# Turning base_w on VectorE instead of TensorE in the last expert of a two-layer MoE kernel

## The reference

```python
# layer 0: per-sample 128x128 matrix, then a top-8 of 64 experts MoE (I = 384, capacity 256)
y = einsum('bct,bcd->bdt', x, weights[conditions])
h = silu(inp @ wg[e]) * (inp @ wu[e]);  out = h @ wd[e]        # for each of 64 experts
# layer 1: a dense layer with an adapter, then a dense layer with router and 8 LoRA experts
c = x @ W.T + s[a] * (x @ A[a].T) @ Bm[a].T
f = c @ base_w.T + base_b + 2 * sum_e gate_e * (c @ lora_A[e]) @ lora_B[e],  gate from c @ router_w.T + router_b
```

## Time and profile before

| | |
|---|---|
| median of 3 runs | 2366.0 us (2363.48 to 2366.01) |
| the profiled execution: time, span | 2365.02 us, 2363.3 us |
| PE busy | 2326.7 us, 98% of the span |
| DVE, ACT, POOL busy | 75%, 60%, 57% of the span |
| granted PE clock, mean | 0.995 |
| chain that ended last: PE | 94% of the span |
| experts' period | 25.0 us each |
| composition stage (L931) | 1791.6 to 1907 us |
| DMA | 582 MB, mean 246 GB/s |

### The profile page before, as it was taken

How to read it: one execution, slowest core, us unless ns; L and a number is a source line. 1 busy time by engine, 2 the same in 40 slices (tenths; PEclk the granted TensorE clock), 3 DMA queues, 4 the chain that set the end, 5 groups by cost and what they waited for, 6 DMA issues and landing times.

```text
span 2363.3 us, 35497 instructions
## 1 busy us (share of the span) xinstructions
PE 2326.7 (98%) x12594; PEld 2044.4 (87%) x12594; DVE 1780.2 (75%) x3091; ACT 1418.5 (60%) x2349; POOL 1343.8 (57%) x999
## 2 busy tenths in 40 slices
PE   6989999999999999999999999999999999999999
PEld 4768788888888888888888888888889999999999
DVE  4887788888888888888888888888863267666665
ACT  4766677777767777777777776777763122222221
POOL 4117888777777777877778777787730011111110
PEclk9999999999999999999999999999999999999999
DMA  8999899989999989989899899899886444544452
GB/s 300 380 311 335 257 281 288 287 272 292 279 289 290 281 276 283 286 280 279 276 291 282 275 285 279 281 282 287 274 255 140 103 110 131 144 131 132 132 140 83
DMA packets 250307, 582.35 MB, mean 246 GB/s; under 512 B 82697, under 2 KB 106634, under 8 KB 250130
## 3 DMA queue, kind: packets, MB, share of 16 engines
q1 hardware_dynamic: 183154, 401.18, 51.6%
q0 software_dynamic: 55584, 160.02, 26.2%
q10 hardware_dynamic: 11392, 18.88, 2.1%
HBM read 456.25 MB, written 123.45 MB: 245 GB/s over the span
## 4 chain that ended last, share of the span: by engine, by line
PE 94%; DVE 2%; issue 2%; ACT 1%; DMA 1%; ACTq 0%; POOL 0%; SPq 0%; DVEq 0%; POOLq 0%
PE ps L861 26%; PE ps L874 22%; PE ps L860 13%; PE ps L986 9%; PE ps L979 7%; PE ps L931 5%; PE ps L857 4%; PE ps L730 2%; PE ps L969 2%; PE ps L858 2%; PE ps L740 1%; PE ps L943 1%; PE ps L753 1%; PE ps L752 0%; ACT HR L1215 0%
## 5 line engine op out<-in xcount | busy, mean ns | idle before, releaser
L861 PE MATMUL ps<-XX,HR 128*128 128x512 f32 x2688 | 959.7, 396 | 0.0
L632 POOL DMA_INDIRECT Xg<-yd,idx x504 | 659.3, 1308 | 161.1 <-issue 152.7
L860 PE MATMUL ps<-XX,LR 128*128 128x256 f32 x2688 | 750.4, 279 | 0.1
L1747 DVE TENSOR_TENSOR LR<-raw,HR 128x1536 fp32r<-128x1536 f32 x384 | 657.8, 1751 | 10.1 <-ACT HR L1215 9.1
L861 PEld LDWEIGHTS ps<-XX,HR 128*128 128x128 f32 x2688 | 505.1, 188 | 104.2
L1215 ACT ACTIVATE HR<-raw 128x1536 fp32r<-128x1536 f32 x384 | 557.0, 1478 | 22.5 <-DMA raw<-in_L_ffn_wd 17.5
L860 PEld LDWEIGHTS ps<-XX,LR 128*128 128x128 f32 x2688 | 507.6, 189 | 18.3 <-DVE LR L1747 0.7
L654 POOL DMA_INDIRECT accd<-ot,toki x128 | 252.9, 1976 | 150.0 <-ACT ot L1269 127.8
L874 PE MATMUL ps<-LR,hH 128*128 128x512 f32 x768 | 303.3, 395 | 0.0
L874 PE MATMUL ps<-HR,hH 128*128 128x512 f32 x768 | 299.8, 390 | 3.0 <-DVE hL L1793 2.2
L874 PE MATMUL ps<-HR,hL 128*128 128x512 f32 x768 | 301.8, 393 | 0.0
(11 more groups left out here) (252 smaller groups left out, 3869.1 us busy)
## 6 DMA issues: line engine op xcount, KB each, us to landing
raw<-in_L_ffn_wd SPq DMA_DIRECT2D x128, 768.0 KB
raw<-in_L_ffn_wg SPq DMA_DIRECT2D x126, 768.0 KB
raw<-in_L_ffn_wu SPq DMA_DIRECT2D x126, 768.0 KB
yd<-yrow ACTq DMA_DIRECT2D x32, 512.0 KB
x<-accd SPq DMA_DIRECT2D x32, 512.0 KB, 3.9
out<-x SPq DMA_DIRECT2D x31, 512.0 KB, 5.2
xt<-in_x SPq DMA_DIRECT2D x25, 512.0 KB
accd<-xt SPq DMA_DIRECT2D x25, 512.0 KB
```

The costliest lines, as they stand in the source:

```text
L632: eng.indirect_dma_start(Xg[:, c, q, :], None, yd4, bass.IndirectOffsetOnAxis(ap=idx4[:, e % 4, i:i + 1], axis=0))\
L860: eng.matmul(bank(out, 0, CAP), wl, xx[:, 0:CAP], start=False, stop=False)
L861: mm = eng.matmul(bank(out), wh, xx, start=False, stop=(k == 7))
L1747: eng.tensor_tensor(LR[:, (n + 2) % NHL, :], raw[:, n % NRAW, :], HR[:, (n + 2) % NHL, :].bitcast(F32), ALU.subtract).then_inc(s_L, 1)
```

## The change

base_w is no longer turned by PE. SP loads each of its eight row blocks in four DMAs of 32 partitions (rows of 1 KB), DVE turns each block with one stream transpose (32x32 blocks, as the token stage does), and the same order of the contraction index is given to W, Bm, lora_A and router_w by splitting their loads in the same way. The first four row blocks are loaded into Xg and XR, right behind the last expert's last weights; the landings are waited for in pairs of blocks (`d_bw[j // 2]` at 128). In the last expert DVE turns blocks 0 to 3 ahead of split dB and of the join of block 189, blocks 4 and 5 ahead of join 190, blocks 6 and 7 ahead of low_w(0) and join 191. High and low parts of whole blocks (128x1024) are written after the last low_h, and the results of expert 63 after the high parts. The first composition block works its columns in thirds (384, 384, 392), each waiting for its own low parts. The composition's banks are swapped with those of the token stage's start. In the token stage the low planes of tile 4 are written before two `low_T`, `take(p, 1)` of the first fast pair before two `turn_r`, and `sums` gets one more wait.

The diff, cut to its core:

```diff
-        BK = {"G1": 0, "G2": 1, "A": 2, "B": 4, "C": 5, "D": 6}
+        BK = {"G1": 4, "G2": 5, "A": 6, "B": 0, "C": 1, "D": 2}
...
+CF = [(0, 384), (384, 768), (768, NX)]
...
+        def base_in(j):
+            if j < 2:
+                return Xg[:, j, :, :].rearrange("p q s -> p (q s)")
+            if j < 4:
+                return XR[:, j - 2, :, :, :].rearrange("p q j t -> p (q j t)")
+            return x1[:, j - 4, :] if j < 6 else x45[:, j - 6, :]
...
+            def load_b(j):
+                for f in range(4):
+                    eng.dma_start(base_in(j)[32 * f:32 * f + 32, :].rearrange("s (q c) -> s q c", q=4),
+                                  base_w[j * P:(j + 1) * P, f * 256:(f + 1) * 256].rearrange("(q s) c -> s q c", q=4))\
+                       .then_inc(d_bw[j // 2], 16)
...
                 load_unit(n)
+                if n == len(units) - 1:
+                    eng.wait_ge(s_vl, 2 * E)
+                    for j in range(4):
+                        load_b(j)
...
-                        eng.dma_start(laR[:, :, e, :],
-                                      lora_A[e].rearrange("(q p) r -> p q r", p=P)).then_inc(d_la, 16)
-                        eng.dma_start(bmR[:, :, e, :],
-                                      Bm[e].rearrange("(q p) r -> p q r", p=P)).then_inc(d_la, 16)
+                        for f in range(4):
+                            p4 = slice(32 * f, 32 * f + 32)
+                            eng.dma_start(laR[p4, :, e, :],
+                                          lora_A[e].rearrange("(f j i) r -> f i j r", f=4, j=8)[f]).then_inc(d_la, 16)
+                            eng.dma_start(bmR[p4, :, e, :],
+                                          Bm[e].rearrange("(f j i) r -> f i j r", f=4, j=8)[f]).then_inc(d_la, 16)
...
-                        eng.dma_start(wr(k)[:, :, 32 * f:32 * f + 32],
-                                      W.rearrange("(q p) d -> p q d", p=P)[:, :, c:c + 32]).then_inc(d_wr[k % 2], 16)
+                        for h in range(4):
+                            eng.dma_start(wr(k)[32 * h:32 * h + 32, :, 32 * f:32 * f + 32],
+                                          W.rearrange("(h j i) d -> h i j d", h=4, j=8)[h][:, :, c:c + 32])\
+                               .then_inc(d_wr[k % 2], 16)
...
-            eng.wait_ge(s_dn, 4 * (E - 1))
-            for j in range(3):
-                load_b(j)
             eng.wait_ge(s_L, len(units) - 2)
-            eng.dma_start(x1[0:NA, 2, :], router_w).then_inc(d_bw[3], 16)
-            load_b(3)
             load_b(4)
+            load_b(5)
+            with nc.allow_non_contiguous_dma(reason="128-byte runs"):
+                for f in range(4):
+                    eng.dma_start(x1[0:NA, 2, :].rearrange("a (j f i) -> a j f i", j=8, f=4)[:, :, f],
+                                  router_w.rearrange("a (f j i) -> f a j i", f=4, j=8)[f]).then_inc(d_rw, 16)
             eng.wait_ge(s_L, len(units))
-            for j in range(5, 8):
-                load_b(j)
+            load_b(6)
+            load_b(7)
             eng.wait_ge(s_bf, 1)
             load_w(0)
-            eng.wait_ge(s_bf, 17)
+            eng.wait_ge(s_bl, 6)
             load_w(1)
+            eng.wait_ge(s_bl, 10)
...
-                        if e == E - 1:
-                            for n in ([o], [4 + 2 * o, 5 + 2 * o], [12 + o])[j]:
-                                turn_b(n)
+                        if e == E - 1 and j == 0 and o == 0:
+                            turn_router()
...
-                if j == 0:
-                    eng.wait_ge(s_bl, 10)
-                    eng.wait_ge(s_out, 4 * E - 1)
+                if j == 1:
+                    eng.wait_ge(s_out, 4 * E)
...
+                if j == 0:
+                    eng.wait_ge(s_gs, 3 * E)
+                    for g, (a, z) in enumerate(CF):
+                        eng.wait_ge(s_bl, (4, 7, 10)[g])
+                        for q in range(8):
+                            for m, (X, Y) in enumerate([(WH, BH), (WH, BL), (WL, BH)]):
+                                mm = eng.matmul(bank(b0 + g, 0, z - a), X[:, 0, q, :], Y[:, q, a:z],
+                                                start=(q == 0 and m == 0), stop=(q == 7 and m == 2))
...
-            for n in range(12):
-                high_b(n)
+            high_router()
+            for j in range(7):
+                high_b(j)
+            eng.activation(BH[:, :, D + NA:NX], laR[:, :, :, :].rearrange("p q a r -> p q (a r)"), ACT.Copy)\
+               .then_inc(s_bh, 1)
+            high_b(7)
             for o in range(4):
                 result(E - 1, o // 2, o % 2)
-                high_b(12 + o)
-            high_b(16)
...
+            def turn_b(j):
+                eng.wait_ge(d_bw[j // 2], 128)
+                if j >= 5:
+                    eng.wait_ge(s_bt, j)
+                eng.transpose(base_t(j), base_in(j)).then_inc(s_bt, 1)
+
+            def low_b(j):
+                eng.wait_ge(s_bh, j + 2 if j < 7 else 10)
+                eng.tensor_tensor(base_dst(BL, j), base_4(j), base_dst(BH, j).bitcast(F32), ALU.subtract)\
+                   .then_inc(s_bl, 1)
...
+                if e == E - 1:
+                    eng.wait_ge(s_dn, 4 * (E - 1))
+                    turn_b(0)
+                    turn_b(1)
+                    turn_b(2)
+                    turn_b(3)
+                    split("dB", e)
                 join(3 * e)
...
                 low_h(3 * e)
-                split("dB", e)
+                if e < E - 1:
+                    split("dB", e)
+                else:
+                    turn_b(4)
+                    turn_b(5)
                 join(3 * e + 1)
...
+                    turn_b(6)
+                    turn_b(7)
                     low_w(0)
                 join(3 * e + 2)
...
-            for n in range(17):
-                eng.wait_ge(s_bh, n + 2)
...
+            eng.wait_ge(s_bh, 1)
+            eng.tensor_tensor(BL[:, :, D:D + NA], bank(0, 0, 64).rearrange("p (q a) -> p q a", q=8),
+                              BH[:, :, D:D + NA].bitcast(F32), ALU.subtract).then_inc(s_bl, 1)
+            for j in range(7):
+                low_b(j)
+            eng.wait_ge(s_bh, 9)
+            eng.tensor_tensor(BL[:, :, D + NA:NX], laR[:, :, :, :].rearrange("p q a r -> p q (a r)"),
+                              BH[:, :, D + NA:NX].bitcast(F32), ALU.subtract).then_inc(s_bl, 1)
+            low_b(7)
...
                 eng.wait_ge(s_xr, 2 * p + 2)
+                if p == ND:
+                    eng.wait_ge(s_sL, 4)
...
             gate_of(3)
+            low_r(4, 0)
+            low_r(4, 1)
+            low_g(3)
             low_T(2)
-            low_g(3)
             low_T(3)
             final(1, "G2")
             final(1, "D")
-            low_r(4, 0)
-            low_r(4, 1)
...
+                take(p, 1)
                 if p == ND:
                     turn_r(t1 + 2)
                     turn_r(t2 + 2)
-                take(p, 1)
```

More of the change, by code:

```diff
@@ L906, in _ @@
                 down(e)
-            turn_b(16)
             for j in range(9):
@@ L925, in _ @@
                 b0 = mbank(j)
[L926 to L932 removed]
+                if j == 0:
+                    eng.wait_ge(s_gs, 3 * E)
+                    for g, (a, z) in enumerate(CF):
+                        eng.wait_ge(s_bl, (4, 7, 10)[g])
+                        for q in range(8):
+                            for m, (X, Y) in enumerate([(WH, BH), (WH, BL), (WL, BH)]):
+                                mm = eng.matmul(bank(b0 + g, 0, z - a), X[:, 0, q, :], Y[:, q, a:z],
+                                                start=(q == 0 and m == 0), stop=(q == 7 and m == 2))
+                else:
+                    for q in range(8):
+                        for m, (X, Y) in enumerate([(WH, BH), (WH, BL), (WL, BH)]):
+                            for g, (a, z) in enumerate(CG):
+                                mm = eng.matmul(bank(b0 + g, 0, z - a), X[:, j % 2, q, :], Y[:, q, a:z],
+                                                start=(q == 0 and m == 0), stop=(q == 7 and m == 2))
                 mm.then_inc(s_m, 1)
```

99 lines of the change are left out of this document (32 added, 67 removed).

## The result

The changed kernel takes 2370.4 us (median of 19 runs, 2366.5 to 2375.8) where the kernel before, on the same chip, takes 2365.4 (19 runs, 2362.1 to 2368.6): a ratio of 1.0023, 95% interval [1.0017, 1.0030]. The forecast was 2369.0 with a range of 2359 to 2374. It is slower by 4.9 us between medians; the forecast's sum was 2.9 slower.

The account below looks back on a forecast made before the run. TensorE, busy for 98% of the span, was taken as the bound. +4.1 (later composition start) and -1.2 (token stage) gave +2.9 on the profiled 2365.02, so 2367.9; with the median 1.0 above the profile, 2369.0, range 2359 to 2374.

Parts of the forecast that it names:

- Part 1: Ahead of the composition: base_w's transposes leave PE, 7.0 us go, and without other waits the composition starts 7.1 earlier.
- Part 3: base_w's loads behind the last expert's weights: the second pair of row blocks lands at 1774.0, bounds 1765.2 and 1776.
- The scatter: Accumulating scatter of expert 62, beside base_w's loads: takes 5.3 us of all engines, added to the second pair's landing.
- Part 4: Last expert: PE stands 9.0 us for join 189; the composition starts 21.7 after the pair, at 1795.7, +4.1.
- The half clock: Third up block after PE's stop: 3.4 us at half speed, 1.7 lost, covered by DVE's later finish.
- Part 5: Token stage reorderings: low_r(4) earlier gives -1.2; the earlier take, between 0 and -0.5, counted as 0.
- Part 6: More small DMAs for lora_A and B rows in experts 16 to 21 and for W: 0, at most +3.
- The sum: Whole kernel: +4.1 for the later composition start and -1.2 for the token stage give +2.9 us.
- A: The forecast case: base_w's second pair lands from 1772.7 to 1776, +1.6 to +4.9 us; chance 0.5.
- B: base_w's loads: 1 KB rows run at the 4 KB rows' rate, pair lands at 1765.2, -5.9 us; chance 0.13.
- C: Last expert: everything covered, base_w's rows there when DVE is free, both pairs by 1763, time 2357.7; chance 0.07.
- D: Composition stage: SP's queue, W's DMAs behind the last scatter, delays the fourth block; +3 on A, 2372; chance 0.3.

Follow-up runs that it names:

- e5_router_first: Changed kernel with VectorE's turns behind the work TensorE waits for, and router_w's DMAs ahead of base_w's blocks 4 and 5; ratio to the kernel before 0.9992.
- e11_w_ahead: e9_high_first with W's third-block high and low parts, and loads of W's blocks 2 and 3, ahead of steps behind the last scatter; ratio to kernel before 0.9968.
- e3: Changed kernel with each base_w block loaded by one DMA with rows of 4 KB instead of four with 1 KB; ratio to the kernel before 0.9985.
- e4: Changed kernel with the first scatter of expert 62 held until base_w's second pair has landed; ratio to the kernel before 1.0018.
- e2: Changed kernel with base_w's first two pairs of blocks issued ahead of the last expert's weights in SyncE's order; ratio to the kernel before 0.9996.
- e7: Changed kernel with low_r(4, 0) and low_r(4, 1) alone put back to their old place in the token stage; ratio to the kernel before 1.0028.
- e10: e9_high_first with each base_w block loaded by one DMA in rows of 4 KB instead of four with 1 KB; ratio to the kernel before 0.9976.
- e9_high_first: e5_router_first with take(p, 1) back behind two turns, high-part products first in the first composition block, blocks 4 to 7 turned singly; ratio to kernel before 0.9984.

## Why the prediction was right, and where it was off

- **Part 1, the transposes leave, 7.1 us**: shown. The composition's first matmul comes 7.0 earlier against the experts in e5_router_first and 7.1 in e11_w_ahead, where 7.5 in all (7.1 and the low parts' 1.0, less some slower blocks) reach the token row.
- **Part 3, the second pair lands at 1774.0**: it was used at 1774.7 (1777.30 less the shift). The step was off by 0.7, within its bounds of 1765.2 and 1776, and the two causes are shown one by one: with rows of 4 KB the wait is 1.6 (e3), without the scatter in between 5.8 (e4). That the sum came so near is in part luck, because two of its terms were off in opposite directions. The scatter was put at 5.3 and was worth 3.7 (e4). Without it the pair was due at 1759.3 + 9.4 = 1768.7 and was used, in e4, at 1771.0 on the same clock, 2.3 later. The prediction gave the queue to the two pairs alone. By 1777.3 the changed kernel had moved 2871 packets under 2 KB since 1759, 354 of them under 512 B, so some 2500 rows of 1 KB, where the pairs are 2048. The other 470 are rows of blocks 4 and 5, issued from 1767.46 on, and take 2.1 us at 73 ns on 16 engines (an estimate from these counts).
- The Trainium skill (DMA: Bandwidth & Descriptors, Queues, rings and completion order) says that an engine drains several descriptors of one queue before it turns. I had taken that as four rows of 1 KB to one packet of the scatter, and the pair at 1772.7. The packets passed one for one instead (last section); whether an engine takes them singly or in equal batches no run here shows. The same page of the Trainium skill gives 512 B as the least size for the full rate (Specifications); for this form of load the packets below contradict it, 72 ns for 1 KB against 142 for 3.3 KB on average.
- **Part 4, PE stands 9.0 us, the composition starts 21.7 behind the pair**: 9.56 and 21.64 (1777.30 to 1798.94). The shape was right: one wait for gu, a turn that starts after a DMA. The half clock was there and was covered. From the end of low_h 191 to the fourth low part I gave 4.4, though the terms beside it (0.2, 1.1, three times 1.18) add up to 4.8; it took 4.3, since ACT's high part began beside the low_h. And I said that only the first column group waits and priced the block at its old 12.72; it took 12.93 (+0.21). That a shortage of VectorE stood behind it, worth 3 us as soon as the rows are in time, I did not see; e5_router_first found it.
- **Part 5, -1.2**: low_r's earlier place gave 1.0, and the take, taken at 0 between 0 and -0.5, cost 0.4, outside the bounds I gave it. The failed step is "low_g then ends at 1984.9, where PE wants it at 1984.5": I moved it by the take's length alone and left out that the take would itself wait for TensorE and that ACT stands between the turns and the low parts. Net -0.6.
- **Part 6, 0**: no wait of TensorE in experts 16 to 21 of the changed kernel's profile (e2, e7 and e10 have one in expert 21), none at W's blocks, though a DMA of W took SyncE 0.58.
- **The sum** by these terms: 2.9 + 0.73 (pair 1) + 0.21 (first block) + 0.6 (token stage) = 4.4, which is the distance's 4.39. The remaining 0.5 to the medians' 4.9 is less than their error (0.0006 of ratio is 1.4 us).
- **Rivals.** A came true at the upper end of its +1.6 to +4.9. B's condition is false here (72 ns for 1 KB), but it was a good counterfactual: forecast 8.8 below A, measured 8.9 in the ratio and 6.6 in the distance by e3. Against the kernel before it promised -5.9, and e3 shows -2.2 by the distance (-3.5 by the ratio), since TensorE still stood 1.6, 1.6 and 1.2 behind VectorE. C is what the better orders make of the change; it needed no earlier rows, only later turns. D's stall of TensorE was absent here, although its price per DMA (0.58) was past the 0.55 from which I let it decide. The failed term is the end of expert 63's scatter, put at 1817: ACT's first copy of the stage starts at 1814.78, that is 1812.2, and the fourth block's planes were ready at 1833.6 for a block that starts at 1837.3 (timelines of ACT and VectorE, chain of waits):

```profile
1814.78 0.90 ACT L1413 ACTIVATE MH<-ps,scp 128x768 fp32r<-128x768 f32 x1 [8.68 <-DMA accd<-ot,toki]
...
1832.40 1.23 DVE L1928 TENSOR_TENSOR WL<-x,WH 128x1024 fp32r<-128x1024 f32 x1 [5.12 <-ACT WH L1297]
...
1837.31 0.87 PE ps L932 x8
```

  e9_high_first shows the same path as waits of 0.8 and 1.0, and e11_w_ahead takes them away.
- The chance for slower by over 0.2% was 0.33, for the same 0.47. The measured 0.23% is at that border, and the interval reaches to both sides.

## What to carry to other kernels

Work moved off the bounding engine comes back as a wait if its data lands after the place where it was put in the helper's in-order queue: put it as late as its reader allows, not as early as its buffer does. Here the form of the transfer then stopped mattering (6.6 us in one order, 0.2 in the other). After each stall that goes, read the chain of waits again; here four stood behind one another (base_w's rows, router_w's rows, VectorE's low parts, and the last scatter with the stores and W's loads behind it), and the size of each was hidden until the one before it had gone. What a reordering cost here was what the moved step itself waited for, plus the hand-over behind it, and not its length. And a sum that comes out right can hold two wrong terms: only the run that takes one of them away (e4) shows it.

## What the hardware showed

Windows of the changed kernel around TensorE's stop (columns as above):

```profile
1772.00:1776.00 4.00, 0.41 (x3) 0.09 (x1) 0.00 (x0) 0.00 (x0) 0.00 (x0) 0.93 1.05 245
1776.00:1780.00 4.00, 0.00 (x0) 0.00 (x0) 2.70 (x3) 0.00 (x0) 0.00 (x0) 0.50 1.13 213
1780.00:1782.00 2.00, 0.04 (x1) 0.04 (x1) 1.91 (x2) 0.06 (x1) 0.00 (x0) 0.50 0.11 22
1782.00:1785.00 3.00, 3.00 (x10) 2.62 (x11) 2.02 (x4) 1.26 (x3) 0.00 (x0) 0.50 0.80 204
1785.00:1787.00 2.00, 2.00 (x11) 1.74 (x11) 1.81 (x2) 0.16 (x1) 0.00 (x0) 0.83 1.03 208
```

TensorE stops at 1772.4. The granted clock goes to 0.50 (1.2 GHz) while it stands, and is back at 1.00 (2.4 GHz) some 3.7 us after it resumes at 1781.96 (0.83 on average over the last two us), near the 3.4 of the earlier trace rows.

Packets, from the DMA queues of the changed kernel: first 1764.5 to 1774 (9.5 us, 16 engines), then its two parts, 1764.5 to 1768.5 ahead of the scatter's packets and 1769 to 1774 beside them:

```profile
q1 hardware_dynamic: 1192, 1.08, 56.2%
q0 software_dynamic: 263, 1.00, 52.7%
...
q1 hardware_dynamic: 913, 0.83, 108.5%
q0 software_dynamic: 6, 0.02, 3.1%
...
q0 software_dynamic: 237, 0.89, 89.4%
q1 hardware_dynamic: 243, 0.23, 16.6%
```

and of e3_rows_4k, 1748 to 1757 (9 us):

```profile
q1 hardware_dynamic: 902, 2.98, 88.9%
```

A packet of the queue with base_w's 1 KB rows takes 16 x 9.5 x 0.562 / 1192 = 72 ns over the whole stretch (73 in the estimate), an accumulating packet of 4 KB 16 x 9.5 x 0.527 / 263 = 304 ns, and the queue with 4 KB rows 142 ns for 3.3 KB on average. While both queues have work they pass packets one for one, 237 against 243, as in the earlier trace rows with 280 against 334. Between two accumulating packets of 302 ns stands one small one, so the queue of 1 KB rows falls from 228 packets a us to 49. Those 243 packets would have taken 1.1 us by themselves, so the scatter's 5.0 us put the pair back by some 3.9 (an estimate), and e4_scatter_held measured 3.7. SyncE's issue of the same DMA form is not one number either: 0.48 us each for the first eight and 0.66 for the next eight.
